# The order of small steps on three engines at four places of a graph and mixture network, one core

## What is computed

```python
x = x + _L0_gnn_ref(_layernorm(x), ...);  x = x + _L0_ffn_ref(_layernorm(x)[None], ...)[0]
x = x + _L1_gnn_ref(_layernorm(x), ...);  x = x + _L1_ffn_ref(_layernorm(x)[None], ...)[0]
x = x + _L2_gnn_ref(_layernorm(x), ...);  x = x + _L2_ffn_ref(_layernorm(x)[None], ...)[0]
x = x + _L3_gnn_ref(_layernorm(x), ...);  x = x + _L3_ffn_ref(_layernorm(x)[None], ...)[0]
```

```python
logits = xf @ router_w.T
top_logits, top_idx = jax.lax.top_k(logits, K)
top_w = jax.nn.softmax(top_logits, axis=-1).astype(x.dtype)
for e in range(E):
    w_e = jnp.sum(top_w * (top_idx == e), axis=-1)
    h = jax.nn.silu(xf @ Wg[e].T) * (xf @ Wu[e].T)
    out = out + h @ Wd[e].T * w_e[:, None]
```

## Time and profile before

| | us |
|---|---|
| median of 3 runs | 1196.97 |
| lowest, highest | 1196.62, 1197.96 |
| the profiled execution, its own time | 1195.46 |
| its span, first to last instruction | 1193.70 |
| TensorE busy in it | 1136.3 (95%) |
| VectorE, ScalarE busy | 582.1 (49%), 458.2 (38%) |
| weight transfers, share of the DMA engines' time | 86.2% |

### The profile page before, as it was taken

How to read it: one execution, slowest core, us unless ns; L and a number is a source line. 1 busy time by engine, 2 the same in 40 slices (tenths; PEclk the granted TensorE clock), 3 DMA queues, 4 the chain that set the end, 5 groups by cost and what they waited for, 6 DMA issues and landing times.

```text
span 1193.7 us, 15702 instructions
## 1 busy us (share of the span) xinstructions
PE 1136.3 (95%) x6347; PEld 716.9 (60%) x6347; DVE 582.1 (49%) x892; ACT 458.2 (38%) x525; POOL 22.4 (2%) x48
## 2 busy tenths in 40 slices
PE   7899999899999999989999999999999999889988
PEld 5666785776755455536776686565665555445533
DVE  7877744756644334203565774454544532232310
ACT  4855614533533233102362464353434432222210
POOL 2000010000000000000000000000000000000000
PEclk9999999999999999999999999999999999999999
DMA  9998565957999999999775498999999999999996
GB/s 374 421 411 348 195 242 217 386 202 305 426 424 425 426 425 424 424 421 418 291 296 205 167 421 333 428 425 427 423 426 425 425 426 425 425 426 425 425 423 269
DMA packets 45368, 443.15 MB, mean 371 GB/s; under 512 B 5088, under 2 KB 5248, under 8 KB 11888
## 3 DMA queue, kind: packets, MB, share of 16 engines
q1 hardware_dynamic: 42336, 427.05, 86.2%
q0 software_dynamic: 2960, 15.09, 3.2%
HBM read 441.73 MB, written 0.39 MB: 370 GB/s over the span
## 4 chain that ended last, share of the span: by engine, by line
PE 72%; DMA 13%; SPq 5%; DVE 4%; ACT 4%; issue 1%; POOL 0%; DVEq 0%; ACTq 0%
PE PJ L2040 14%; PE PJ L2009 10%; DMA scratch<-in_weights 10%; PE AC L2077 8%; PE TP L2099 6%; PE PJ L2018 5%; SPq L647 5%; DMA ring<-in_weights 4%; PE AC L1836 3%; PE AC L1824 2%; PE PJ L2000 2%; PE TP L2050 2%; PE MS L1637 2%; PE PJ L1770 1%; PE TP L1968 1%
## 5 line engine op out<-in xcount | busy, mean ns | idle before, releaser
L2040 PE MATMUL PJ<-ring,picked 128*64 128x512 f32 (+1 forms) x588 | 149.7, 594 | 0.0
L915 ACT ACTIVATE low<-PJ 128x512 f32<-128x512 f32 x51 | 30.3, 594 | 242.0 <-PE PJ L2040 169.5
L1395 DVE SCALAR_TENSOR_TENSOR act<-low,CB,PJ 128x512 f32<-128x512 f32 x51 | 38.0, 746 | 159.3 <-PE PJ L2009 84.1
L2040 PE MATMUL PJ<-scratch,picked 128*32 128x512 f32 (+1 forms) x360 | 106.9, 594 | 2.2 <-DMA extra<-in_weights 2.2
L2099 PE MATMUL TP<-ring,extra 128*64 128x512 f32 (+3 forms) x384 | 102.4, 488 | 3.0 <-issue 2.6
L1413 DVE TENSOR_TENSOR ring_lo<-ring,w_lo_u 128x1536 fp32r<-128x1536 f32 x40 | 69.2, 1756 | 52.9 <-ACT w_lo_u L932 52.9
L2099 PE MATMUL TP<-scratch,extra 128*64 128x512 f32 (+3 forms) x320 | 86.4, 489 | 0.4 <-DMA ring<-in_weights 0.4
L932 ACT ACTIVATE w_lo_u<-ring 128x1536 fp32r<-128x1536 f32 x40 | 58.3, 1486 | 67.3 <-DMA ring<-in_weights 30.9
L2040 PEld LDWEIGHTS PJ<-ring,picked 128*64 128x64 f32 (+1 forms) x588 | 42.7, 124 | 55.6 <-issue 54.9
L1413 DVE TENSOR_TENSOR ring_lo<-ring,w_hi_u 128x1536 fp32r<-128x1536 f32 x34 | 58.8, 1755 | 20.8 <-ACT w_hi_u L932 20.4
L932 ACT ACTIVATE w_hi_u<-scratch 128x1536 fp32r<-128x1536 f32 x26 | 37.5, 1482 | 77.5 <-DMA scratch<-in_weights 61.7
(11 more groups left out here) (467 smaller groups left out, 2246.3 us busy)
## 6 DMA issues: line engine op xcount, KB each, us to landing
ring<-in_weights SPq DMA_DIRECT2D x147, 1536.0 KB, 18.1
scratch<-in_weights SPq DMA_DIRECT2D x73, 1536.0 KB, 20.1
extra<-in_weights SPq DMA_DIRECT2D x39, 1536.0 KB, 21.9
extra<-in_attn POOLq DMA_DIRECT2D x11, 768.0 KB, 10.4
ring<-in_weights SPq DMA_DIRECT2D x8, 768.0 KB, 29.9
extra<-in_attn POOLq DMA_DIRECT2D x6, 512.0 KB, 10.6
extra<-in_weights SPq DMA_DIRECT2D x4, 768.0 KB, 25.1
ring<-in_weights SPq DMA_DIRECT2D x8, 384.0 KB, 16.7
```

Of the source, the lines that this page charges most:

```text
L915: A(silu, PJ[:, 0:SEG], ACT.Silu).then_inc(S("silu_ready"), 1)
L1395: v.scalar_tensor_tensor(hexp, silu, weight, PJ[:, SEG:2 * SEG], ALU.mult, ALU.mult) \
L2040: ins = mm(dst[c], x[:, t, c], slab_at(LOAD[q, kind, side])[:, t * SEG:(t + 1) * SEG], start=(t == 0), stop=(t == KT - 1))
```

## The change

It has four parts. In the two mixtures, ScalarE rounds one half of the second pass's gate slab ahead of the copies of the turned tokens and the other half behind them; the two halves of the up slab both stand behind the router's exponent. TensorE's count of the choices moves from behind three of the first pass's gate tiles to behind one in the first mixture, and from behind two to ahead of all in the second. In layer 2's feed-forward layer, VectorE makes one low half ahead of the weighting of the hidden values and not two. In the fourth graph layer, ScalarE copies the first projection ahead of the next slab's high halves, VectorE makes the terms of that projection ahead of the low halves, and ScalarE runs one exponent of a constant column (`exp_of_power`, used by nothing) right behind the copies of the tokens.

```diff
--- before.py
+++ after.py
@@ -358,6 +358,7 @@
         veps = sb("veps", [P, 2])
         rstd = sb("rstd", [P, 2])
         power = sb("power", [P, 1])
+        exp_of_power = sb("exp_of_power", [P, 1])
         al = sb("al", [P, 2, HEADS])
         hmax = sb("hmax", [P, HEADS])
         hneg = sb("hneg", [P, HEADS])
@@ -871,12 +872,14 @@
                 for t in range(n + 3):
                     if c == 2 and t < 2:
                         narrow_split_hi(t + 2)
-                    if c == 5 and t < 2:
-                        graph_split_hi(t + 2, (0,))
+                    if c == 5 and t == 1:
+                        graph_split_hi(3, (0,))
                     if t < n:
                         copy_h(c, t)
-                    if c == 5 and t < 2:
-                        graph_split_hi(t + 2, (1,))
+                    if c == 5 and t == 0:
+                        graph_split_hi(2)
+                    if c == 5 and t == 1:
+                        graph_split_hi(3, (1,))
                     if 0 <= t - 3:
                         segment_turned(c, t - 3)
                     if 0 <= t - 2 < n:
@@ -931,14 +934,14 @@
                             act.wait_ge(S(name), value)
                         A(hi_half(n, half), half_slab(n, half), ACT.Copy).then_inc(S("whole_hi"), 1)
 
-                whole_hi(first + 1, "g")
+                whole_hi(first + 1, "g", (0,))
                 transposed(k)
                 A(XTh[:].rearrange("p (h k) n -> p h (k n)", h=2), turned_halves(TP), ACT.Copy) \
                     .then_inc(S("XTh_ready"), 1)
-                whole_hi(first + 1, "u", (0,))
+                whole_hi(first + 1, "g", (1,))
                 act.wait_ge(S("router_shifted"), nth + 1)
                 A(r8[:, 1, :], r8[:, 0, :], ACT.Exp).then_inc(S("router_exp"), 1)
-                whole_hi(first + 1, "u", (1,))
+                whole_hi(first + 1, "u")
                 for q in range(first, LAST_PASS[l] + 1):
                     whole_hi(q - 1, "d")
                     silu_of(q)
@@ -1045,6 +1048,7 @@
             keep_x(6)
 
             transposed(8, XTh[:])
+            A(exp_of_power[:], power[:], ACT.Exp)
             first_narrow(5)
             second(6)
             keep_x(7)
@@ -1322,8 +1326,6 @@
                         narrow_split_lo(2)
                     if c == 2 and t == 1:
                         narrow_split_lo(3, (0,))
-                    if c == 5 and t == 0:
-                        graph_split_lo(2, (0,))
                     if 0 <= t - 1 < n:
                         logits(c, t - 1)
                     if c == 5 and 1 <= t < 3:
@@ -1332,7 +1334,7 @@
                         dve.wait_ge(S("h_copied"), SEG_BASE[c] + t + 1)
                         terms(GAT[c]["unit"] + t, range(t * k, t * k + k), C, h_tile(c, t))
                         if c == 5 and t == 0:
-                            graph_split_lo(2, (1,))
+                            graph_split_lo(2)
                     if 0 <= t - 2 and not FIRST[c]["elu"]:
                         activate(c, t - 2)
                         narrow_segment_lo(t - 2)
@@ -1612,11 +1614,12 @@
             then(v.tensor_copy(r8[:, 2, :], MS[:, 0:E8]))
             then(top2(r8[:, 2, :], r8[:, 4, :]))
             then(v.tensor_tensor(comb, r8[:, 2, :], r8[:, 4, :], ALU.mult))
-            graph_split_lo(0)
+            graph_split_lo(0, (0,))
             dve.wait_ge(S("l2_gelu"), 1)
             g3 = G2.rearrange("p (e f) -> p e f", e=E8)
             v.tensor_tensor(g3, g3, comb.unsqueeze(2).to_broadcast([P, E8, F2]), ALU.mult) \
                 .then_inc(S("l2_weighted"), 1)
+            graph_split_lo(0, (1,))
             graph_split_lo(1)
 
             layernorm(7, X[:], 9, 6)
@@ -1995,7 +1998,7 @@
                         n = LOAD[q, kind, 0]
                         landed(pe, n)
                         for t in range(KT):
-                            if between and t == {1: 3, 3: 2}[l]:
+                            if between and t == {1: 1, 3: 0}[l]:
                                 between()
                             ins = mm(dst, XT[:, t, :], slab_at(n)[:, t * SEG:(t + 1) * SEG], start=(t == 0),
                                      stop=(t == KT - 1))
```

## The result

| | us | against before |
|---|---|---|
| forecast | 1197.4 (1194.6 to 1198.9) | 1.0003 |
| median of 20 runs (1196.85 to 1201.82); before beside them 1196.80 | 1199.23 | 1.0020, interval 1.0012 to 1.0028 |
| the same kernel once more, 12 runs (1196.09 to 1200.65); before 1196.23 | 1197.45 | 1.0012, interval 1.0002 to 1.0022 |
| its profiled execution; span | 1198.96; 1197.2 | |

The change makes the kernel slower: the medians differ by 2.4 us in the first measurement and by 1.2 in the second. The ratio and its interval are worked out from the single runs, so a ratio need not be the quotient of the two medians beside it (1.0012 is 1.4 us). The forecast was no change (+0.4). Its range ended 0.3 us under the first median; the second median lies inside it, 0.05 us from the forecast.

A forecast was written before the change was run, and what follows sets the result against it. Bounds: the load stream (first mixture), the dependent chain (549 to 676 us), TensorE's start of unbroken work (second mixture). Terms -0.2 - 0.25 - 0.2 + 1.06 = +0.4 us gave a median of 1197.4 us, range 1194.6 to 1198.9.

The forecast's parts named there:

- The order on three engines: Both mixtures: VectorE's unchanged order holds router's copy and choice by 1.44 us; TensorE waits at the count, SP for the order.
- The rival that the copy isn't held: Both mixtures: the router's copy is not held, -2.05 us, so 1194.9, or 1193.9 with the copies' whole lead; chance 0.16.
- Layer 2 and the graph layer: Layer 2: weighting starts 0.25 us sooner; fourth graph layer: copy starts at 605.7, not 606.45, VectorE's work 0.2 us sooner.
- the held start: Second mixture: TensorE stands at least 1.05 us at the count, so its unbroken work moves by +1.06 us.
- are 1.1 and 1.5 us and would have to double: Both mixtures: TensorE's new waits judged too short for a clock fall, after pauses of 3.55 us (fall) and 3.09 (none).
- that rival: TensorE's clock falls to 1.2 GHz in the new wait: 1.7 us on top of +0.4, so 1199.1; chance 0.06.
- The first mixture: First mixture (l = 1): the experts' order, and the load stream with it, gains 0.2 us; TensorE's delay is covered by loads.
- the cover: First mixture: TensorE's lag of 1.7 us is hidden by the loads; were the cover gone, up to 1.7 would be lost.
- The sum: Whole kernel: -0.2 - 0.25 - 0.2 + 1.06 = +0.4 us.
- the bound of 2.9 us: First mixture: a slab may be given up 2.9 us later before the stream breaks, from landing times 9.2 and 6.3 us.
- the forecast's lag of 1.5 us: First mixture: TensorE starts its second product at 271.42 and not 269.54, +1.5 us after the count's 0.37.

The follow-up runs named there:

- the half slab alone: Kernel before with only ScalarE's half slab moved behind the copies of the turned tokens in both mixtures, counts as before: 0.9997.
- the third, with the same stand and a full clock: Kernel before with the half slab behind the copies and the count ahead of all products, in the second mixture alone: 1.0015, 1198.23 us.
- the kernel with eight products: Changed kernel with 8 products of the identity ahead of the count's wait in the second mixture: 1.0002, 1197.44 us.
- the kernel with the count behind two: Changed kernel with the second mixture's count back behind two products, as in the kernel before: 0.9991, 1194.88 us.
- The two held ones without any fall in the mixture: Changed kernel with the second mixture's count back behind two products, 0.9991; changed kernel with 6 products of the identity ahead of that count, 1.0002.
- the count alone: Kernel before with only the second mixture's count moved ahead of all products of the first gate pass: 1.0004, 1196.81 us.
- layer 2 and the graph layer alone: Kernel before with only the edits in layer 2 and the fourth graph layer, both mixtures as before: 0.9989, 1195.39 us.

## Why the prediction was wrong

**The order on three engines: right.** The choice was held by 269.38 to 271.99 less the 1.20 us of the transposes, 1.41 (forecast 1.44), and by 3.03 - 1.55 = 1.48 in the second mixture. The first count came 0.96 - 1.20 = -0.24 (forecast -0.2). TensorE stood 1.83 and 1.52 us. The rival that the copy isn't held is refuted.

**Layer 2 and the graph layer: right.** The low half is 588.65 - 586.57 = 2.08 later than before, the weighting 1.83: -0.25, as forecast. The copy of the first projection moved by 1.03 where the projection moved by 1.82 (-0.79, forecast -0.75), TensorE's wait for the terms by 1.53 (-0.29, forecast -0.2), and its length grew from 0.72 to 0.81.

**The second mixture: the failed step.** The forecast term was +1.06 for the held start, with nothing for the clock. The traces without a fall show +1.19 to +1.29 for a held start, those with one +2.95 and +2.96. The step that failed is the sentence that the new waits "are 1.1 and 1.5 us and would have to double" for the clock to fall. It set a bound between the pauses of the earlier trace rows, 3.09 and 3.55 us. In the runs the clock fell to 1.2 GHz behind 1.52 us in two of three traces. The bound was not even good for its own place: the pause at some 1072 us is 3.05 to 3.7 us long in all 17 traces, and in 13 of them the clock falls in it or within 1.2 us behind it. The trace of before is one of the other four. With the half slab alone, in the timeline and the busy table:

```profile
1073.98 1.01 PE L2077 MATMUL AC<-w_hi_u,extra_lo 128*128 128x512 f32 x2 [3.10 <-DVE extra_lo L1421]
```

```profile
1073.80:1076.90 3.10, 2.92 (x9) 2.54 (x10) 3.10 (x3) 1.15 (x1) 0.00 (x0) 0.50 1.01 428
```

The pause is 0.01 us longer than before, and here the clock falls; one execution can't set such a bound.

This entry differs from the place of the earlier trace rows: ahead of the stand lie transposes, products 8 columns wide and products of the identity with small pauses, and behind it two counts; whether that is why a shorter stand was enough isn't shown. The price of that rival was right (1.7; measured 2.95 - 1.26 = 1.69), and its chance of 0.06 was too low. That its time, 1199.1, is the first median to 0.1 us is in part luck: it has nothing for the first mixture, which took 0.6 to 0.9 longer in the traces, and the second median is 1197.45. The Trainium skill (TensorE: Matmul & The Clock Gate, "What's actually happening") has the throttled clock as the default that activity lifts; the two traces agree, and the third, with the same stand and a full clock, shows that the stand's length alone doesn't decide.

**The first mixture: the cover held just so, its end did not.** The forecast term was -0.2, the traces show +0.89 and +0.60. The loads landed at 1.1 to 1.4 us later than before from 276 to 549 us, which is the offset of 1.20: a lag of 1.5 us is covered. How far the cover reaches is seen in the kernel with eight products, where the clock fell behind the stand of the first mixture as well; with a lag of 3.3 us the loads were some 1.8 us later from 340 us on, and the mixture took 1.67 longer. Its busy table there:

```profile
272.40:275.70 3.30, 3.30 (x5) 1.24 (x5) 2.88 (x15) 1.08 (x1) 0.00 (x0) 0.50 0.00 0
```

So of a lag of 3.3 us some 1.5 were covered. By this one trace the bound of 2.9 us, taken from two times to landing, was about twice too wide, and the forecast's lag of 1.5 us had next to no room left. What I left out is the last slab. Before, and in the kernel with the count behind two, whose timeline this is, TensorE waits for it:

```profile
549.43 0.64 PE L2102 MATMUL TP<-ring,extra 128*64 128x512 f32 x1 [0.42 <-DMA scratch<-in_weights]
551.39 1.53 PE L2160 MATMUL AC<-extra,picked 128*128 128x512 f32 x4 [0.46 <-DVE extra L1508]
```

The stream sets the end by these 0.4 us only. In the changed kernel's timeline no such wait is left, and its busy table has a granted clock of 0.50 some 20 us ahead:

```profile
553.32 1.53 PE L2160 MATMUL AC<-extra,picked 128*128 128x512 f32 x4 [0.45 <-DVE extra L1508]
```

```profile
527.90:531.20 3.30, 3.30 (x8) 1.08 (x10) 0.00 (x0) 0.00 (x0) 0.00 (x0) 0.50 1.01 417
```

A fall at 527 us, behind a wait of 2.17 us for a landing, ate it up. Of the eight traces in which TensorE stands in the first mixture, five have this fall (+0.60 to +1.01 us for the mixture); of the nine other kernels' traces, before among them, one has it, and one more a fall at 519. The two held ones without any fall in the mixture have -0.06 and +0.28, near the -0.2 of the forecast. Whether the lag brings the fall, or chance, isn't shown.

**The sum.** By the first trace +0.89 - 0.25 - 0.28 + 2.95 = +3.3 us up to the second pass, against +0.4; by the second +0.60 - 0.25 - 0.28 + 2.96 = +3.0. From there to the end the two traces give back 1.0 and 2.1 us against that of before; with the count alone, whose code is the same there, 1.6 were given back too, with the half slab alone nothing, with layer 2 and the graph layer alone 1.2. So that part differs as widely between traces whose code is the same there. The medians, +2.4 and +1.2, lie under the traces' sums, which fits falls that come in some executions and not in others. In how many the clock falls at the second entry isn't shown: the mean granted clock of the changed kernel, 0.9929 and 0.9939 in its two measurements against 0.9945 for before, makes by estimate some 1.1 and 0.4 falls more than before, at all places together (a fall of 3.4 us takes 0.0014 off it, see below).

## What to carry to other kernels

When two engines do a job in halves, move the halves on both: a half that one engine puts off holds everything that stands behind its counterpart in the other's order. Before a wait is put ahead of TensorE's work, ask whether TensorE arrives there first; if so, leave some real products ahead of it, or the stand costs itself (1.2 us here) and in some executions the clock (1.7). A pause that did no harm in one trace is weak evidence: the one of 3.09 us of before came with a fall of the clock in 13 of 17 traces, and a shorter one at another place (1.52) did so in two of three.

## What was not expected of the hardware

**Falls of the clock differ from execution to execution of one kernel.** The granted clock, as the mean over an execution, was 0.989 to 0.999 in 143 executions of the kernel before, 0.9945 in the mean. One fall of 3.4 us to 0.50 takes 0.5 x 3.4 / 1195 = 0.0014 off it, so by this estimate four falls are usual, and the traced execution, at 0.999, was among those with the fewest. That fits its lying 1.5 us under the median, and it makes one trace a poor witness of where the clock holds.

**A column given its place ahead of other tiles in SBUF changes the time of a product.** Groups of TensorE's instructions at 745 to 1000 us, the kernel before, then with the one column ahead of other tiles (the last number before the idle time is the mean of one in ns):

```profile
L2009 PE MATMUL PJ<-w_hi_u,XTh 128*128 128x512 f32 x66 | 26.1, 395 | 0.0
L2018 PE MATMUL PJ<-ring_lo,XTh 128*128 128x512 f32 x60 | 23.9, 398 | 0.0
L2077 PE MATMUL AC<-w_lo_u,extra_lo 128*128 128x512 f32 x40 | 15.3, 400 | 0.0
```

```profile
L2010 PE MATMUL PJ<-w_hi_u,XTh 128*128 128x512 f32 x66 | 25.8, 391 | 0.0
L2019 PE MATMUL PJ<-ring_lo,XTh 128*128 128x512 f32 x60 | 23.4, 390 | 0.0
L2078 PE MATMUL AC<-w_lo_u,extra_lo 128*128 128x512 f32 x40 | 15.5, 405 | 0.0
```

The instructions are the same, and the places of the tiles behind the column are all that the edit moves; some got 4 to 8 ns shorter, others 5 longer. TensorE gained 1.14 us between 677 and 1000 us by it, and the trace of every kernel with the column shows the same means. As the loads set the end there, the time didn't change.
